# Attention and mixture-of-experts block: queries of two batches made together in high and low parts, inputs one batch further ahead

## The reference

```python
def attention(x, latents, shift, scale, ...):        # x: ctx_1024, latents: layernorm(x)
    x = layer_norm(x, ln1_w, ln1_b)
    lat = layer_norm(latents, ln2_w, ln2_b)
    lat = lat * (1.0 + scale[:, None, :]) + shift[:, None, :]
    q = jnp.einsum('bld,ed->ble', lat, Wq)           # 256 -> 1024, 16 heads of 64
    kv_in = jnp.concatenate((x, lat), axis=-2)       # 256 keys for each batch
    kv = jnp.einsum('bld,ed->ble', kv_in, Wkv)       # 256 -> 2048
    ...
    w = jax.nn.softmax(logits, axis=-1)
    out = jnp.einsum('bhqk,bhkd->bhqd', w, v)
    return jnp.einsum('ble,de->bld', out, Wo)
x = x + attention(ctx_1024, layernorm(x), cond_1024, cond_1024, ...)
x = x + experts(layernorm(x), ...)
```

## Time and profile before

| | |
|---|---|
| median of three runs | 706.17 us (705.66 to 709.35) |
| the profiled execution | 707.77 us, its span 706.0 us, so 1.8 us lie around the span |
| TensorE busy | 689.7 us of the span |
| VectorE, ScalarE, GpSimd busy | 474.6, 439.8 and 255.9 us |
| granted TensorE clock, mean | 0.998 of full speed |

### The profile page before, as it was taken

One profiled execution on the slowest core, in us unless ns is written; L12 is line 12 of the kernel. 1 busy time (PEld: TensorE's weight loads), 2 busy tenths in 40 slices (PEclk: granted clock), 3 DMA queues, 4 the chain that ended last, 5 costly groups with the idle time before them and its releaser, 6 DMA issues. The chain is left out here.

```text
span 706.0 us, 18044 instructions
## 1 busy us (share of the span) xinstructions
PE 689.7 (98%) x6037; PEld 640.1 (91%) x6038; DVE 474.6 (67%) x993; ACT 439.8 (62%) x1208; POOL 255.9 (36%) x406
## 2 busy tenths in 40 slices
PE   7899999999999999999999999999999899999997
PEld 7789999899899998999989978898889899999997
DVE  5878888887877878888888675366545655333343
ACT  4787887887878878788787875242344544223232
POOL 4924223232332321422546541057131344423333
PEclk9999999999999999999999999999999999999999
DMA  8343444444444343444445433004557976767660
GB/s 296 95 124 96 123 112 115 117 107 115 112 125 109 98 134 106 108 124 104 117 118 137 116 81 127 1 0 117 163 204 267 326 284 231 274 234 273 224 256 12
DMA packets 54473, 103.80 MB, mean 147 GB/s; under 512 B 12700, under 2 KB 32926, under 8 KB 51744
## 3 DMA queue, kind: packets, MB, share of 16 engines
q1 hardware_dynamic: 44336, 85.80, 39.4%
q0 software_dynamic: 7072, 14.71, 7.5%
q10 hardware_dynamic: 3024, 2.76, 1.3%
HBM read 59.81 MB, written 12.74 MB: 103 GB/s over the span
## 5 line engine op out<-in xcount | busy, mean ns | idle before, releaser
L915 PE MATMUL PS<-BIG 128*128 128x256 f32 (+1 forms) x1164 | 196.0, 322 | 0.6 <-issue 0.4
L915 PEld LDWEIGHTS PS<-BIG 128*128 128x128 f32 x1164 | 166.1, 189 | 14.8 <-issue 1.0
L1908 PE MATMUL PS<-XST,W 128*128 128x128 f32 x1012 | 118.4, 277 | 1.9 <-issue 1.9
L582 ACT ACTIVATE PR<-PS,NMX 128x256 f32<-128x256 f32 x256 | 117.8, 475 | 2.9 <-DVE NMX L740 2.8
L1908 PEld LDWEIGHTS PS<-XST,W 128*128 128x128 f32 x1012 | 116.5, 194 | 2.2 <-issue 2.1
L591 ACT ACTIVATE PR<-PR,RINV 128x256 f32<-128x256 f32 x256 | 105.9, 517 | 0.4 <-DVE RINV L747 0.4
L752 DVE STREAM_TRANSPOSE PR<-PR 128x512 f32<-128x512 f32 x124 | 80.6, 687 | 2.5 <-ACT PR L591 2.0
L437 POOL DMA_DIRECT2D PT<-PR x128 | 64.6, 510 | 44.0 <-DVE PR L752 37.3
L740 DVE TENSOR_REDUCE NMX<-PS 128x4 f32<-128x1024 f32 x64 | 75.4, 1197 | 1.8 <-PE PS L973 1.8
L935 PE MATMUL PS<-KVF,WQ 128*128 128x128 f32 x512 | 65.6, 281 | 1.6 <-DVE BIG L728 1.1
L935 PEld LDWEIGHTS PS<-KVF,WQ 128*128 128x128 f32 x512 | 59.6, 192 | 7.0 <-issue 5.0
(11 more groups left out here) (190 smaller groups left out, 1192.7 us busy)
## 6 DMA issues: line engine op xcount, KB each, us to landing
W<-in_w SPq DMA_DIRECT2D x21, 1408.0 KB, 5.9
PT<-PR SPq DMA_DIRECT2D x368, 64.0 KB, 2.0
PT<-PR POOLq DMA_DIRECT2D x128, 64.0 KB, 2.4
W<-in_w SPq DMA_DIRECT2D x8, 640.0 KB, 4.0
xs_sorted<-ZERO SPq DMA_DIRECT2D x26, 128.5 KB, 3.1
W<-in_w SPq DMA_DIRECT2D x8, 352.0 KB, 3.4
XS<-xs_sorted ACTq DMA_DIRECT2D x21, 128.5 KB, 2.8
RC<-in_ctx SPq DMA_DIRECT2D x16, 128.0 KB, 2.7
```

Source lines behind the costliest of these rows:

```text
L582: last = act.activation(probs, logits, ACT.Exp, bias=NMX[:, g, own, p % 2:p % 2 + 1], accum_out=SUM[:, p, own:own + 1])
L915: last = pe.matmul(dst, stat(s, k), mov(m, k), start=n == 0, stop=n == len(todo) - 1)
L1908: last = pe.matmul(h[:, P * c:P * (c + 1)], lhs13(W13[par], k, c), XST[par][:, k, :], start=k == 0, stop=k == KD - 1)
```

## The change

Batches 2 to 15 have their queries made in pairs: batches n and n + 1 (n even) share the weight loads, as one moving operand of two blocks of 128 columns, in high and low parts (`q_pair_unit`, 12 matmuls of 256 columns for two head pairs of two batches, called twice for each half, g = 0 and 1). That happens in the second half of odd batches and the first half of even ones (`pair_made`); the other halves make no queries. Only batches 0 and 1 keep `q_unit`. Each unit fills bank `PROJ[0]`; `output_projection` stands behind the second one now, between the two `v_unit`s. For this the inputs run one batch further ahead: `modulate` is for b + 2, `norm_stats` for b + 3, and `KV` has four slots. Batch 0 makes up the difference: VectorE gets `norm_stats(2)`, `norm_rows(2)` and `norm_again(2)` into half 0, and `modulate(2)` into half 1. `WQ` is split in parts by GpSimd in batch 1 (`wq_split`). The room comes from a tensor `RAWBIG` laid over `BIG`: raw weights of the experts and of the queries, `KVF`, `CN` and `XN` now lie where low and high parts will be written later, and the raw expert weights `ws13` are loaded near batch 13 rather than at the start.

```diff
+        def pair_made(b, H, par):
+            if par == 1 and H == 1 and not (isinstance(b, int) and b == NB - 1):
+                return b + 1
+            if par == 0 and H == 0 and not (isinstance(b, int) and b == 0):
+                return b
+            return None
...
+            def wq_split(H):
+                part = slice(INNER // 2 * H, INNER // 2 * (H + 1))
+                pool.wait_ge(d_wq, 16)
+                for k in range(KD):
+                    pool.tensor_copy(WQS[0][:, k, part], WQ[:, k, part]).then_inc(p_wqh, 1)
+                    pool.wait_ge(p_wqh, KD * H + k + 1)
+                    pool.tensor_tensor(WQS[1][:, k, part], WQ[:, k, part], WQS[0][:, k, part].bitcast(FP32),
+                                       ALU.subtract).then_inc(p_wql, 1)
...
                 if not first:
                     keep_probs(b - 1, 1)
+                if isinstance(b, int) and b == 1:
+                    for H in range(2):
+                        wq_split(H)
                 early = 0 if not between else HP if not first else HP + 2
                 for j in range(early):
                     between(j)
-                if following:
-                    kv_lo(b + 1, 1 - par)
+                if first:
+                    norms(2)
+                    kv_lo(1, 1)
+                elif following:
+                    kv_lo(b + 2, (slot + 2) % SLOTS)
...
                 exps(h, b, H, 0, final)
                 if not final:
-                    if not ahead:
-                        q_hi(h + 1, 1 - H)
+                    if isinstance(b, int) and (b, H) in SINGLE:
+                        q_hi(*SINGLE[b, H])
+                    if n is not None:
+                        q_pair_hi(n, 1 - H, 0)
                     k_hi(h + 1, 1 - H, 0)
                 exps(h, b, H, 1, final)
                 if not final:
                     k_hi(h + 1, 1 - H, 1)
                 for p in (2, 3):
                     exps(h, b, H, p, final)
+                if n is not None:
+                    q_pair_hi(n, 1 - H, 1)
...
                 inverse_sums(h, 1)
+                if n is not None:
+                    q_pair_lo(n, 1 - H, 1)
                 if not first:
                     residual(b - 1, H)
...
+                if first and H == 0:
+                    norm_stats(2)
+                    norm_rows(2)
+                    norm_again(2)
                 if H == 1 and norm:
-                    norm_again(b + 2)
+                    if first:
+                        norm_rows(3)
+                    norm_again(b + 3)
                 if not final:
                     for p in (2, 3):
                         transpose_blocks(h, H, p)
...
+            def q_pair_unit(n, H, g, slot):
+                if g == 0:
+                    if H == 0:
+                        pe.wait_ge(p_kvl, n + 2)
+                        pe.wait_ge(v_out, n - 1)
+                    else:
+                        pe.wait_ge(v_sum, n - 1)
...
+                else:
+                    pe.wait_ge(v_q, q_count(n, H, 0) - 1)
+                x = PAIRS[slot // 2]
+                for j in range(2):
+                    e = 128 * (HP * H + 2 * g + j)
+                    last = split3(pairs_bank()[:, :, P * j:P * (j + 1)],
+                                  lambda s, c: WQS[s][:, c, e:e + 128], lambda m, c: x[m][:, :, c, P:KEYS], range(KD))
+                last.then_inc(t_q, 1)
...
                 if not final:
-                    if not (first and H == 0):
-                        q_unit(h + 1, nb, nH, npar)
+                    if isinstance(b, int) and (b, H) in SINGLE:
+                        q_unit(*SINGLE[b, H])
+                    if n is not None:
+                        q_pair_unit(n, nH, 0, nfirst)
                     for i in range(2):
-                        k_unit(h + 1, nb, nH, npar, i)
-                    if H == 0 and not last:
-                        transpose_inputs(b + 1)
-                    if not first:
+                        k_unit(h + 1, nb, nH, nslot, i)
+                    if n is not None:
+                        q_pair_unit(n, nH, 1, nfirst)
+                    if first:
+                        transpose_inputs(H + 1)
+                    elif H == 0 and not (isinstance(b, int) and b >= NB - 2):
+                        transpose_inputs(b + 2)
+                    if not first and n is None:
                         output_projection(h - 2, b - 1, H)
                     if first and H == 0:
                         pe.wait_ge(p_wv_lo, 4)
                 for tile in range(2):
-                    v_unit(h, H, par, tile, final=final)
+                    v_unit(h, H, slot, tile, final=final)
+                    if tile == 0 and n is not None:
+                        output_projection(h - 2, b - 1, H, made=n)
```

More of the change, by code:

```diff
@@ L34 @@
 HP = NP // 2
-LOOPS = (NB - 4) // 2
+SLOTS = 4
+assert NB % SLOTS == 0
 EPS = 1e-5
@@ L501, in _ @@
             batch(0, 0, first=True, between=wo_split)
-            with pool.Fori(0, LOOPS) as i:
-                batch(2 * i + 1, 1)
-                batch(2 * i + 2, 0)
+            batch(1, 1)
+            with pool.Fori(0, 2) as i:
+                for n in range(SLOTS):
+                    batch(SLOTS * i + 2 + n, (2 + n) % SLOTS)
+            for b in range(2 + 2 * SLOTS, NB - 3):
+                batch(b, b % SLOTS)
             pool.wait_ge(d_rt, 16)
@@ L629, in half, with batch @@
                         v_all(h, H, tile)
-            def batch(b, par, first=False, last=False):
-                half(b, 0, par, first, last)
-                half(b, 1, par, first, last)
+            def batch(b, slot, first=False, last=False):
+                half(b, 0, slot, first, last)
+                half(b, 1, slot, first, last)
             def keys_hi(H):
@@ L659, in _ @@
             batch(0, 0, first=True)
-            with act.Fori(0, LOOPS) as i:
-                batch(2 * i + 1, 1)
-                batch(2 * i + 2, 0)
-            batch(NB - 3, 1)
-            batch(NB - 2, 0)
-            batch(NB - 1, 1, last=True)
+            batch(1, 1)
+            with act.Fori(0, (NB - SLOTS) // SLOTS) as i:
+                for n in range(SLOTS):
+                    batch(SLOTS * i + 2 + n, (2 + n) % SLOTS)
+            batch(NB - 2, (NB - 2) % SLOTS)
+            batch(NB - 1, (NB - 1) % SLOTS, last=True)
             tail_hi(0)
@@ L828, in half @@
                     inverse_sums(h, 0)
-                elif norm:
-                    norm_rows(b + 2)
+                elif norm and not first:
+                    norm_rows(b + 3)
                 inverse_sums(h, 1)
+                if n is not None:
+                    q_pair_lo(n, 1 - H, 1)
                 if not first:
@@ L875, in _ @@
             batch(2, 0)
-            with dve.Fori(0, LOOPS - 1) as i:
+            with dve.Fori(0, (NB - 8) // 2) as i:
                 batch(2 * i + 3, 1)
                 batch(2 * i + 4, 0)
-            batch(NB - 3, 1)
-            batch(NB - 2, 0, norm=False)
-            batch(NB - 1, 1, last=True, norm=False)
+            for b in range(NB - 5, NB):
+                batch(b, b % 2, last=b == NB - 1, norm=b < NB - 3)
             for p in (0, 1, 2):
@@ L972, in logits @@
                         for own in range(2):
[L973 removed]
+                            last = pe.matmul(twos(LG[p // 2][own])[:, p % 2, :], q[OWN[own], place, p, :], k[OWN[own], j, :],
                                              start=n == 0, stop=n == 2)
```

287 lines of the change are left out of this document (180 added, 107 removed).

## The result

The changed kernel takes 725.38 us (median of five runs, 724.51 to 726.82), the kernel before 705.73 in the same comparison: a ratio of 1.027 (95% interval 1.024 to 1.030), slower. I had said 715.5.

What follows compares the result with a forecast made beforehand. TensorE was taken to bound the kernel. Work less wait 2.8 us slower, batch 0 5.4 and rescaling beside `kv_lo` 1.1 summed to 9.3 us on 706.17: 715.5 us, forecast 711 to 719 (wider range 706.5 to 720).

Steps and rivals of the forecast that it cites:

- TensorE's work: Paired queries, batches 2 to 15: 24 matmuls at 2.86 us replace two query units, saving 10.4 us in all.
- The wait at the projection: Query-making halves: TensorE waits 1.01 and 0.56 us for the second unit's low part; with restarts 13.2 us over seven pairs.
- The start: Batch 0: the norm of batch 2 delays the last two transposes and next `row_max`, costing 5.4 us, between 3 and 7.
- collision: VectorE's rescaling of batches 2 and 3 beside GpSimd's `kv_lo`: 0.54 us twice, 1.1 us more, bounds 0 and 2.6.
- VectorE's lag into a short half: VectorE's queued `residual` and transposes end about 3.0 us into the next half, against 2.8 before; the lag does not grow.
- rival (d): Short halves: probabilities reach `times_v` late, 0.6 us beyond the margin in each of 12, giving 722.5 us; chance 13%.
- no wait ahead of `times_v` in the loop: Sign expected in the profile after: in the loop, TensorE does not wait for probabilities before `times_v`.
- over 52: Sign against the forecast: four halves, forecast at 51.3 us, taking over 52 us (or under 50.6) would show it wrong.

Runs made afterwards that it cites:

- b_loop4_pe: The kernel before, with a loop body of four batches instead of two on TensorE alone: ratio 1.0050, 709.2 us on the scale.
- a_moves8: The changed kernel with a half's 16 probability moves split 8 to SyncE and 8 to GpSimd instead of 12 and 4: ratio 1.0283, 725.7 us.
- b_loop4: The kernel before, with loop bodies of four batches instead of two on TensorE, ScalarE and GpSimd: ratio 1.0060, 709.9 us on the scale.
- a_best: The changed kernel with earlier second rounding, 10 and 6 moves, batch 2's norm taken apart in batch 0, TensorE's loop written out: ratio 0.9930, 700.8 us.

## Why the prediction was wrong

**Right.** TensorE's work: the 24 query matmuls take 1.51 + 1.36 = 2.87 us by their starts (forecast 2.86). The wait at the projection: 0.98 to 1.07 and, in all first halves but (14,0), 0.48 to 0.53 us (forecast 1.01 and 0.56), and removing its cause gave 12.4 us by the trace (forecast 13.2). The two leave 3.8 us instead of 2.8: most of the pairs' halves take 14.77 where I had 14.73, (1,1) takes 14.93 and (14,0), without its transposes, waits 1.07. The start was right in kind: `row_max` came 6.45 us late, of which I had 5.4 and a collision. VectorE's lag into a short half, which I put at 3.0 us though the terms written out sum to 2.8, was 2.95 (`row_max` at 198.13, logits at 195.18).

**Wrong: the probabilities.** The step that failed is the margin in rival (d): 8.9 us after the last transpose against 9.3 asked for, from a queue time of 7.50 and a landing of 2.0. I gave it 13% and wrote "no wait ahead of `times_v` in the loop". The 9.3 was right: 9.4 by the timelines around (6,1). The 8.9 was not: the earlier trace rows came from a stretch without instruction fetches. The changed kernel has them, and the moves took 8.14 to 8.74 us in all six places, the slowest landing 2.7 to 3.4 us after its issue. That used up the 0.4 us and cost 5.2 in all. The trace of before had such moves too, outside the stretch that I read; its queue timeline:
```profile
80.02 8.34 SPq L333 DMA_DIRECT2D PT<-PR  x12
...
360.00 8.69 SPq L333 DMA_DIRECT2D PT<-PR  x12
```
That 5.2 is near the 7 of rival (d) is chance. I had 0.6 us in each of 12 short halves. But of these only six can wait so, (3,0), (5,0) and on to (13,0): between making and use of their probabilities lies a short half, for the other six a long one. Those six waited 0.87 us each in the mean. My condition ("over 52") shows it: four halves took 52.36.

**Left out: the loop.** The change makes TensorE's body four batches instead of two. I took the code's length as free. It costs 2.5 us at the jumps and is what made (d) come true; b_loop4_pe shows the stalls and the slow issues in the kernel before, whose halves are too long for a wait to come of them.

**Too small: the start.** 5.4 + 1.1 = 6.5 us were forecast, 7.6 measured. The term that was mis-sized is the collision: beside a `kv_lo` the rescaling took 1.34 and 1.35 us, 0.93 more than alone and not 0.54. I had read the price off a neighbour of 256 columns where `kv_lo` has 512. The rule of the Trainium skill ("SBUF — State Buffer", Who interferes with whom), which I had priced at all of a `kv_lo`, some 1.3 us, each time, was as far off on the other side. Here GpSimd began 0.06 and 0.08 us ahead, and the rescaling ended 0.15 us behind it. In the earlier trace rows VectorE began first and still ended 0.15 us behind. So the trace agrees that the rescaling is held up for nearly the whole GpSimd operation, but it does not show the one issued first going first. The rest, 0.4 us, no run took apart. In half (0,1) `modulate(2)`, `norm_rows(3)`, a wait for the root and the second collision all stand ahead of the last two transposes, so `row_max` of (1,0) came 9.4 us late (51.44 instead of 42.02), and TensorE waited at the projection of (1,0). VectorE's and TensorE's timelines:
```profile
48.95 1.35 DVE L814 TENSOR_SCALAR RAWBIG<-RAWBIG,MV,RS 128x256 f32<-128x256 f32 x1 [0.82 <-POOL RS L485]
```
```profile
55.04 0.36 PE L1048 MATMUL PS<-WOH,OTH 128*128 128x256 f32 x1 [0.81 <-DVE QL L840]
```

3.84 + 5.20 + 7.63 + 2.53 = 19.20. The forecast had 9.3 of it; 7.7 come from the loop's length and the probabilities, the other 2.2 are the 1.0 of the long halves and the 1.1 of the start.

## What to carry to other kernels

A margin of a few tenths of a microsecond is read from a queue and a landing as they are now; ask what in the change alters the queue itself, and price the case where the margin is gone. Longer loop bodies aren't free: look in the DMA view for instruction packets inside the loop, before and after. And a change that brings less work but puts its last step late on a neighbour may lose all of it: here one rounding ahead of one pair's exponentials, two more moves on the second queue, the norm of batch 2 taken apart and TensorE's loop written out turned 2.7% slower into 0.7% faster; but a repair that loads another engine (GpSimd in a_moves8) can give back all that it wins.

## What the runs showed of the hardware

Instruction fetches cost an engine that isn't short of instructions itself. SyncE's issue of a 64 KB move, 591 ns in the median, took 1.0 to 2.1 us when one fell into it, and a landing 3.4 instead of 2.6 us. The DMA view tells two queues of fetches apart, and only one of them does this. In the 14 traces, from 38 to 420 us, a fetch of queue 8 began within 0.3 us of a move's start 167 times, and 148 of these moves took 1.0 us or more; 148 moves met a fetch of queue 14 alone, and none did. With TensorE's body alone lengthened (b_loop4_pe) the loop from 143 to 348 us has 18 packets on queue 8 and none on 14; with all three bodies (b_loop4) 19 and 9. So queue 8 goes with TensorE's code. How a fetch holds up another engine's issue, no run shows.

TensorE's jump back over a body of four batches left it idle 0.90 to 1.68 us, in ten traces. Over two batches no such idle time showed, and between 136 and 352 us no fetch. One iteration leaves 1,988 instructions of TensorE in the trace of the changed kernel and 2,061 in b_loop4_pe, where the two batches of the kernel before leave 1,032. The Trainium skill ("Runtime: NRT & Kernel Launch", Instruction fetch mechanics) says that TensorE's store holds 2048 instructions and that a taken branch to code that is no longer in it waits for a fetch. The jumps here agree in kind: the long bodies lie near that number, one a little under it and one over, and the short one far below; where the limit is, no run shows. The page would have warned me of the loop.

TensorE's clock fell after it had been idle at the start: in the changed kernel it was busy 2.06 of the 5.86 us ahead of 35.60 us, and then, in the windows view,
```profile
35.60:39.94 4.34, 4.33 (x25) 4.34 (x26) 3.89 (x6) 1.93 (x7) 4.18 (x8) 0.64 0.27 60
```
the granted clock was 0.64, between the level of 2.4 GHz and that of 1.2, and the 24 matmuls of the keys took 4.49 us where 3.12 is usual. It was covered there, since the unit behind them waited for VectorE anyway. In a_best it isn't: behind 1.63 us idle in the 5.39 ahead of 37.36 us, a unit of values took 4.61 instead of 2.90 us, in the same view of a_best,
```profile
37.36:41.90 4.54, 4.54 (x12) 3.31 (x13) 3.59 (x11) 4.54 (x15) 2.95 (x7) 0.62 0.67 177
```
and that is part of what the start still costs.
